# Attention and quantised linear layer on one core: sets loaded at the start of a unit and copied at its end, and the two tiles of an odd unit prepared in two key blocks

## The reference

```python
xn = _layernorm(x)                                   # per token, 256 features
q = (xn @ Wq.T).reshape(n, s, 16, 16)
k = repeat((xn @ Wk.T).reshape(n, s, 8, 16), 2)      # two query heads share a key head
v = repeat((xn @ Wv.T).reshape(n, s, 8, 16), 2)
energy = einsum('nqhd,nkhd->nhqk', q, k) + alibi     # alibi = -|i - j| * 2**-(h+1)
attn = softmax(energy / sqrt(16))
attention = einsum('nhqk,nkhd->nqhd', attn, v).reshape(n, s, 256) @ Wo.T + bo
x_scale = maximum(max|xn|, 1e-6) / 127               # per token
x_q = clip(round(xn / x_scale), -128, 127)           # int8
linear = (x_q @ Wq8.T) * x_scale * weight_scale + bias
result = x + attention + linear
```

## Time and profile before

| | |
|---|---|
| median of 3 runs | 1682.9 us (1679.3 to 1685.19) |
| profiled execution, its own time | 1682.93 us |
| its span in the profile | 1681.1 us |
| TensorE busy (matmul) | 1512.6 us, 90% |
| VectorE busy | 1412.1 us, 84% |
| ScalarE busy | 1187.3 us, 71% |
| GpSimd busy | 1058.1 us, 63% |
| TensorE's mean granted clock | 0.976 of full speed |
| DMA queue q1 | 138.27 MB, 31.7% of 16 engines |

### The profile page before, as it was taken

How to read it: one execution, slowest core, us unless ns; L and a number is a source line. 1 busy time by engine, 2 the same in 40 slices (tenths; PEclk the granted TensorE clock), 3 DMA queues, 4 the chain that set the end, 5 groups by cost and what they waited for, 6 DMA issues and landing times.

```text
span 1681.1 us, 41787 instructions
## 1 busy us (share of the span) xinstructions
PE 1512.6 (90%) x15948; PEld 572.1 (34%) x15948; DVE 1412.1 (84%) x1729; ACT 1187.3 (71%) x2331; POOL 1058.1 (63%) x1596
## 2 busy tenths in 40 slices
PE   6799899999998899898899998999989899898889
PEld 5233332333332333332333333333333333232223
DVE  5889889898888898798898888889888888797881
ACT  3467777677777676677676776767777777676776
POOL 5467777677778676667676676767677675332222
PEclk8999999999999999999999999999999999999999
DMA  7423223333323333233333233333233332211221
GB/s 170 106 62 86 72 76 85 94 89 93 95 71 93 91 87 92 79 89 84 102 85 89 78 85 90 101 81 98 84 84 84 98 80 67 62 53 51 57 56 58
DMA packets 197288, 140.94 MB, mean 84 GB/s; under 512 B 107040, under 2 KB 165728, under 8 KB 197088
## 3 DMA queue, kind: packets, MB, share of 16 engines
q1 hardware_dynamic: 197088, 138.27, 31.7%
HBM read 81.40 MB, written 35.63 MB: 70 GB/s over the span
## 4 chain that ended last, share of the span: by engine, by line
PE 57%; DVE 26%; issue 11%; SPq 4%; DMA 3%; POOL 0%; ACT 0%; DVEq 0%; POOLq 0%; ACTq 0%
DVE row_max L968 23%; PE ps_ring L1248 18%; PE ps_pv L1324 17%; PE ps_row L1265 12%; PE ps_ring L1360 4%; PE ps_ring L1380 3%; DVE pv_turned L1008 1%; PE ps_ring L1363 1%; SPq L454 1%; DMA k<-k_alibi 1%; SPq L458 1%; PE ps_ring L1374 1%; DMA token_dram<-token 1%; PE ps_row L1352 1%; DVE att_normed L1024 0%
## 5 line engine op out<-in xcount | busy, mean ns | idle before, releaser
L968 DVE TENSOR_REDUCE row_max<-ps_row 128x1 f32<-128x1024 f32 x1024 | 1205.6, 1214 | 192.6 <-PE ps_row L1267 182.3
L1140 ACT ACTIVATE probs<-ps_ring 128x512 f32<-128x512 f32 x2048 | 1087.0, 600 | 358.0 <-PE ps_ring L1248 357.0
L733 POOL TENSOR_TENSOR probs<-probs,near 128x256 f32<-128x256 f32 x512 | 374.2, 731 | 459.8 <-ACT probs L1140 451.0
L1248 PE MATMUL ps_ring<-q,k 122*32 122x512 bf16 x8192 | 645.0, 389 | 6.5 <-DMA q<-neg_max_t 5.7
L1324 PE MATMUL ps_pv<-probs,v_unit 128*32 128x512 f32 x4096 | 543.2, 607 | 0.0
L1265 PE MATMUL ps_row<-k,q 64*128 64x512 bf16 x1000 | 347.5, 389 | 138.6 <-issue 80.7
L1248 PEld LDWEIGHTS ps_ring<-q,k 122*32 122x32 bf16 x8192 | 214.3, 96 | 538.9 <-ACT probs L1140 296.8
L1267 PE MATMUL ps_row<-k_again,q_again 64*128 64x512 bf16 x1000 | 348.2, 390 | 0.0
L1265 PEld LDWEIGHTS ps_row<-k,q 64*128 64x128 bf16 x1000 | 86.4, 93 | 446.2 <-issue 291.4
L1324 PEld LDWEIGHTS ps_pv<-probs,v_unit 128*32 128x32 f32 x4096 | 127.3, 111 | 48.3 <-issue 2.7
L1008 DVE STREAM_TRANSPOSE pv_turned<-ps_pv 128x512 f32<-128x512 f32 x64 | 45.9, 717 | 49.6 <-PE ps_pv L1324 49.6
(11 more groups left out here) (83 smaller groups left out, 962.8 us busy)
## 6 DMA issues: line engine op xcount, KB each, us to landing
parts_dram<-parts SPq DMA_DIRECT2D x59, 288.0 KB, 3.7
q_again<-q SPq DMA_DIRECT2D x63, 256.0 KB, 3.1
token_b<-token_dram SPq DMA_DIRECT2D x53, 256.0 KB, 3.8
q<-parts_dram SPq DMA_DIRECT2D x128, 96.0 KB
k<-parts_dram SPq DMA_DIRECT2D x256, 32.0 KB
q<-parts_dram SPq DMA_DIRECT2D x128, 64.0 KB
att_dram<-att_unit SPq DMA_DIRECT2D x126, 64.0 KB
att_t<-att_dram SPq DMA_DIRECT2D x56, 128.0 KB, 2.9
```

The costliest lines, as they stand in the source:

```text
L733: pool.tensor_tensor(here, here, near[:, u % KV_HEADS, :].rearrange("p (e n) -> p e n", e=GROUP), ALU.mult).then_inc(weighted, 1)
L968: dve.tensor_reduce(row_max[:, par, e, qb:qb + 1], ps_row[qb % 2][:, :], AX_X, ALU.max, negate=True).then_inc(row_max_found, 1)
L1140: act.activation(probs[:, c % PBUFS, e, h * HALF:(h + 1) * HALF], ring_bank(u, c, e, h), ACT.Exp, scale=SCALE).then_inc(ring_freed, 1)
L1248: mm = pe.matmul(to[at, :], weights[:, at], moving, start=start, stop=stop)
```

## The change

In SP's `unit`, `load_set(u + 3)` moves from the end of unit u to its beginning (`next_set`), and `load_again(u + 3)` follows it at the end of the same unit, so one unit ahead of where it was. A set whose last tile is made in unit u itself (`late_set`, units 8, 16, ... 56) is still loaded at the end, its copies come a unit later, and its first head's row blocks run as `row_block`, without the copies.

In an odd unit, the even tile stays in key block 1 and the odd tile goes to key block 3 (`prep_at`): TensorE's outputs and qkv, ScalarE's moves, half of VectorE's layer norm and statistics. GpSimd's `split_high` and `split_middle` of the odd tile go from key blocks 2 and 3 to 4 and 5, and SP's `store_parts` of it goes behind `place_max`. VectorE's `turn_pv` goes from behind reduction 2 to behind reduction 3.

```diff
+def last_tile(u):
+    return BLOCKS * (u // KV_HEADS + 1) - 1
+def late_set(u):
+    return u >= SETS - 1 and last_tile(u) >= PREP_AHEAD and made_unit(last_tile(u)) == u - SETS + 1
+def prep_at(t):
+    return 1 if t % PAIR != PREP_AHEAD % PAIR else 3
...
             def unit(u, f):
-                if u > 0 and u + 2 < UNITS:
-                    load_again(u + 2, (u + 2) % SETS)
                 if f["next_x"]:
                     next_x(u + X_AHEAD)
                 if f["xt"]:
                     load_xt(u + 2 + PREP_AHEAD)
+                if f["row_set"] and not late_set(u + 3):
+                    next_set(u + 3)
                 if u % PAIR == 1:
                     store_att(u - 1)
                 for t in f["normed"]:
                     store_token(t)
                 for t in f["made"]:
-                    store_parts(t, t % 2)
+                    if prep_at(t) == 1:
+                        store_parts(t, t % 2)
...
                 if not f["last"]:
                     place_max(u + 1, (u + 1) % SETS)
+                for t in f["made"]:
+                    if prep_at(t) == 3:
+                        store_parts(t, t % 2)
                 if f["prev"] and u % PAIR == 0:
                     store_att(u - 1)
                 for t in f["next_att"]:
                     load_att_t(t, t % 2)
                 if f["row_set"]:
-                    tiles = u + PREP_AHEAD if u % PAIR == 1 else max(u - 1 + PREP_AHEAD, PREP_AHEAD)
-                    wait_parts(min(tiles, TILES), 0)
-                    if u > 0:
-                        wait_filled(sp, u - 1, BLOCKS - 1, GROUP - 1, 1)
-                    load_set(u + 3, (u + 3) % SETS)
+                    if late_set(u + 3):
+                        next_set(u + 3)
+                    else:
+                        load_again(u + 3, (u + 3) % SETS)
+                if u + 2 < UNITS and late_set(u + 2):
+                    load_again(u + 2, (u + 2) % SETS)
                 for t in finished(u):
                     store_out(t, t % 2)
+            def next_set(u):
+                wait_parts(last_tile(u) + 1, 0)
+                if u >= SETS:
+                    wait_filled(sp, u - SETS, BLOCKS - 1, GROUP - 1, 1)
+                load_set(u, u % SETS)
...
                     if c == 1:
-                        for made in f["made"][:1]:
-                            split_high(made)
-                            split_middle(made)
-                    if c == 2:
-                        for made in f["made"][1:]:
-                            split_high(made)
+                        for made in f["made"]:
+                            if prep_at(made) == 1:
+                                split_high(made)
+                                split_middle(made)
+                    if c == 4:
+                        for made in f["made"]:
+                            if prep_at(made) == 3:
+                                split_high(made)
                     if c == 3 and not f["last"]:
                         split_max(u + 1)
-                    if c == 3:
-                        for made in f["made"][1:]:
-                            split_middle(made)
+                    if c == 5:
+                        for made in f["made"]:
+                            if prep_at(made) == 3:
+                                split_middle(made)
...
-                        if i == 2 and f["prev"]:
+                        if i == 3 and f["prev"]:
                             turn_pv(u - 1)
...
-                    if c == 1:
-                        for t in f["normed"]:
+                    if c in (1, 3):
+                        for t in f["normed"][c // 2:c // 2 + 1]:
                             normalise(t, t % 2)
                             find_largest(t, t % 2)
                             find_scale(t, t % 2)
-                        for t in f["stats"]:
+                        for t in f["stats"][c // 2:c // 2 + 1]:
                             wait(dve, x_loaded, 16 * (t - X_AHEAD + 1))
                             find_stats(t, t % 2)
...
                 if i < BLOCKS and f["row_heads"] >= 1:
-                    if i == 0 and u == 0:
+                    if i == 0:
                         wait_again(u + 1)
                     half_row_block(u + 1, (u + 1) % SETS, 1, i)
                 if i >= BLOCKS and f["row_heads"] >= 2:
                     if i == BLOCKS:
                         wait_row_set(u + 2, (u + 2) % SETS)
-                        wait_again(u + 2)
-                    half_row_block(u + 2, (u + 2) % SETS, 0, i - BLOCKS)
+                        if not late_set(u + 2):
+                            wait_again(u + 2)
+                    if late_set(u + 2):
+                        row_block(u + 2, (u + 2) % SETS, 0, i - BLOCKS)
+                    else:
+                        half_row_block(u + 2, (u + 2) % SETS, 0, i - BLOCKS)
...
                     col_half(u, c, 1, 1)
-                    if c == 1:
-                        for t in f["proj"] or f["made"]:
+                    for t in f["proj"] or f["made"]:
+                        if prep_at(t) == c:
                             outputs(u, f, t % PAIR)
-                        for t in f["made"]:
+                    for t in f["made"]:
+                        if prep_at(t) == c:
                             qkv_whole(u, t)
```

More of the change, by code:

```diff
@@ L136, in ring_places @@
             items = [(u, c, e, h) for e in range(GROUP) for h in range(2)]
-            if c == 1:
-                items += [(u, "outputs", t % PAIR) for t in f["proj"] or f["made"]]
-                items += [(u, "qkv", t % PAIR) for t in f["made"]]
+            items += [(u, "outputs", t % PAIR) for t in f["proj"] or f["made"] if prep_at(t) == c]
+            items += [(u, "qkv", t % PAIR) for t in f["made"] if prep_at(t) == c]
             for item in items:
```

## The result

The changed kernel takes 1663.1 us (median of four runs, 1662.6 to 1673.6) against 1683.1 before: 0.990 of the time, 95% interval 0.986 to 0.994. So it is about 1% faster, which is clear of the noise but under 2%: 20 us where 52 were forecast. A later set of five runs of the same kernel gave 1669.7 (1667.6 to 1670.8), beside 1679.8 of the kernel before, so 10 us there.

What follows compares the result with a forecast made beforehand. VectorE's 1412.1 us busy was taken as the harder floor, with time lost waiting for row blocks. 1682.9 - 66 (ordinary pairs) - 22 (end pairs) + 36 (late pairs) = 1631 us; range 1576 to 1674.

Steps and rivals of the forecast that it cites:

- Sets first: Loads at a unit's beginning, copies at its end: the wait at i = 8 goes from 20 ordinary pairs, -58 us.
- turn_pv: One reduction later on VectorE, its data is ready by then: -0.7 us a pair, bounds -0.3 and -1.0.
- Two key blocks, and GpSimd: Ordinary pairs: VectorE idle 0.9 us in key block 3 against 0.7 before; GpSimd's later splits cost 0.6.
- evenly fed row blocks: With tiles in two key blocks, row blocks give back about 0.5 us of VectorE's 0.27 us gaps per ordinary pair.
- Late pairs, first wait: Units 8b-2, set loaded at the end: TensorE's wait at i = 8 stays at about 3 us, with its slow clock.
- the strips: Late set's row blocks made in strips without copies: 1.3 us a unit, between 0 and 0.5 a key block.
- Late pairs, second wait: Units 8b-1, i = 0: TensorE waits about 5 us for late copies, VectorE loses 4.2, bounds 0 and 7.
- place_max: Queued on SP behind the moved loads in even units: about 0.8 us of cover, landing 1.25 us, cost nothing.
- B: Rival: late sets arrive in time, parts ready earlier and SP issuing faster; 1579 us, chance 0.17.
- C: Rival: GpSimd becomes the wait, ordinary and late pairs each pay 1.5 us more; 1671 us, chance 0.15.
- D: Rival: place_max late behind the moved loads at the end of every even unit; 1688 us or more, chance 0.10.
- E: Rival: moved loads wait on store_out and copies still miss i = 8, so waits stay; 1680 us, chance 0.06.

Runs made afterwards that it cites:

- sets alone: Changed kernel with the two key blocks and the turn_pv move undone, set loads and copies still moved, late copies last: 1639.4 us, 0.976.
- the two runs without it: Changed kernel with late sets used without copies, 1615.3 us; changed kernel with late sets' copies ahead of place_max on SP, 1618.4 us.

## Why the prediction was wrong

The waits came and went where the prediction had them. Two prices were too small: that of the second wait of the late pairs (28 us of the 43 by which the profiled run misses), which is the step that failed, and that of the two key blocks in ordinary pairs (12 us). By the prediction's own steps:

**Sets first.** Right. The wait at "issue" is gone from all ordinary pairs, and with "sets alone" they are 47.17, where 47.2 had been put for a pair without it.

**turn_pv.** Right in kind and size: -0.7 was put, 47.20 to 46.49 measured.

**Two key blocks, and GpSimd.** 0.2 for the gap in VectorE's work, 0.6 for GpSimd and -0.5 that "evenly fed row blocks" would give back make +0.3; 46.49 against 47.40 is +0.9. This is the miss in ordinary pairs, 0.6 x 20 = 12 us. Of the parts, the gap is worse than put: before the first reduction behind key block 3 VectorE stands

```profile
765.06 2.35 DVE L997 TENSOR_REDUCE row_max<-ps_row 128x1 f32<-128x1024 f32 x2 [1.75 <-PE ps_row L1297]
```

against 0.9, outside the bound of 1.2. GpSimd cost 0.5. The 0.5 to be given back had no row behind it, and less came: in the pair of units 26 and 27 VectorE has five idle stretches of 0.2 to 0.3 us, 1.4 us in all; with the two key blocks alone undone it has six, 1.6 us, and before the change seven, 1.8 us. So the two key blocks give back 0.3. At the end of the program, 42.3 a pair had been put for 43.47; the pairs there still project two tiles, in two key blocks, and cost 42.65 with one.

**Late pairs, first wait.** That the first wait stays was right, partly by luck: the loads were issued by 830.79 where 833.6 had been put, but TensorE came about 2 us earlier too. It waited 2.82 in unit 30 for 3.10 before, and over the seven late units 3.0 on average for 2.5. VectorE loses 5.1 behind it on average, where it lost 3.3; the strips, put at 1.3, are in the difference.

**Late pairs, second wait.** This is the step that failed: the cover that VectorE's lag was to give. The wait's place was right, its price was not. The copies were put at 850.7 and their landing at 854.5; measured are 850.81 and 855.19. TensorE, put at i = 0 at 849.1, came at 847.86, so it stood 7.33 us (6.1 on average over the seven units) and not about 5. The larger error is the cover. VectorE was put "some 2 us behind", without a row for the 2 us, so that it would lose 3 of the 5. It was 0.25 behind. It lost the wait and the time to the first new row block, 7.33 - 0.25 + 0.65 = 7.73, and 1.95 more at the slow clock: 9.7 in unit 31 and 8.2 on average, where 4.2 had been put and 7 was the upper bound. An ordinary unit has 0.3 at these two reductions, so the wait is worth 7.9, which is what the two runs without it show (59.27 to 51.41 and 51.59). Over seven pairs the difference of some 4 us is the 28 by which the late ones miss.

It was not the first wait that took the cover away. With "sets alone" the late units have no first wait, and at i = 0 of unit 31 the rows are

```profile
836.24 0.61 PE L1292 MATMUL ps_row<-k,q 64*128 64x512 bf16 x1 [6.84 <-DMA q_again<-q]
...
827.28 2.31 DVE L994 TENSOR_REDUCE row_max<-ps_row 128x1 f32<-128x1024 f32 x2
836.89 2.35 DVE L994 TENSOR_REDUCE row_max<-ps_row 128x1 f32<-128x1024 f32 x2 [7.30 <-PE ps_row L1294]
840.87 1.23 DVE L994 TENSOR_REDUCE row_max<-ps_row 128x1 f32<-128x1024 f32 x1 [1.62 <-PE ps_row L1294]
```

TensorE stopped at 836.24 - 6.84 = 829.40 and VectorE had work until 827.28 + 2.31 = 829.59: 0.19 us of cover, and 8.9 lost. In most ordinary pairs, before and after the change, VectorE's last reduction ends 0.37 us after TensorE has come to this place. So the 2 us were never there. The trace before the change could have told: at i = 8 of unit 30 TensorE's wait of 3.10 cost VectorE all of that and more.

```profile
838.13 1.23 DVE L968 TENSOR_REDUCE row_max<-ps_row 128x1 f32<-128x1024 f32 x1 [3.23 <-PE ps_row L1267]
...
842.11 4.73 DVE L968 TENSOR_REDUCE row_max<-ps_row 128x1 f32<-128x1024 f32 x4 [1.17 <-PE ps_row L1267]
```

**place_max** in even units was in time, as put; beyond the first units there is one wait of 0.5 us for it. Its landing, put at 1.25 us, was too short, though. With the copies ahead of it TensorE waited for it in six late units, 0.4 to 2.0 us, and went on 3.2 to 3.9 us after its last issue. So it was in part luck that the change pays nothing here.

**The rivals.** B did not come about: the set's loads took 823.63 to 830.79 to issue and TensorE had to wait until 835.57. The Trainium skill, "DMA: Bandwidth & Descriptors", section "Issuing engines are not separate DMA queues", has a sequencer's time to start a DMA as usually small relative to the DMA itself. The prediction read its trace as speaking against this, but one by one the trace agrees: a load of the set takes 0.4 to 0.7 us to issue, and the other DMAs for which the profile lists a landing mostly take 2.5 to 4.0. What held the set was that thirteen such issues stand in one queue, 7.2 us in a row. C, D and E did not come about: GpSimd's waits are 6.0 us in 21, `place_max` was in time, and the ordinary waits are gone. What happened is the forecast with two of its terms too small. That 1663.1 lies within the stated range of 1576 to 1674 is no support for it: the range goes so high to take in C, at 1671, which did not happen.

What stays open: the profiled run is 10 us longer than the three others of its set, and a second set lies in between. In two traces the ordinary pairs are the same to 0.02 us and the late ones to 0.3, so where the shorter runs gain isn't shown.

## What to carry to other kernels

When a change moves work ahead for most iterations and leaves exceptions, cost the exceptions as a sequence of their own: here 7 of 30 pairs took back 64 of the 72 us that the other 23 gained, and moving one pair of copies ahead of `place_max` on the same in-order queue was worth 50 us. Cover (the work that a trailing engine still has when the engine ahead of it stops) has to be read from the trace at the place where the wait will stand: 2 us were assumed, and 0.2 to 0.4 were there, with or without a wait before it. Undo each part of a combined change alone: sets and `turn_pv` without the two key blocks, with copies in time, are 1563.8 us, about 100 below the change as it stands.

## What the runs showed of the hardware

After a wait of 7.33 us TensorE's granted clock was 0.50 over the next 3.9 us, so it ran at 1.2 GHz for all of it:

```profile
855.10:859.00 3.90, 3.81 (x24) 0.98 (x28) 2.36 (x2) 0.64 (x2) 0.00 (x0) 0.50 0.34 98
```

In this stretch the eight matmuls of `pv_block` took 1.93 us, where they take 1.03 a key block later, and VectorE lost a further 1.95 us. Behind the shorter wait of 2.82 it lost 1.31. Also, one issue on SP took 1.96 us (k_again at 848.12) where the same instruction took 0.55 at 850.81. It delayed the copies behind it by 1.4 us, and I had no term for that; what held it the trace doesn't show.
